# Batch 0 of a fused two-layer kernel, planned anew: order of loads, two transpose banks, slabs turned one step ahead

## The chip, the cores and the metric

One core of one Trainium2 chip. The time is the device time of one launch in microseconds, as the median of several runs. Beside it stands a profile: one execution recorded by the hardware, whose times count from the start of its span. The engines are PE (TensorE: matmuls and transposes), DVE (VectorE), ACT (ScalarE), POOL (GpSimd) and SP (SyncE, which issues DMAs here). Each runs its own list of instructions in order and waits on semaphores. PEld is TensorE's load of weights, which runs beside its matmuls.

## The reference

```python
def _L0_cond_ref(hidden_states, W, b, coeff, mask):
    output = jnp.einsum('bsi,oi->bso', hidden_states, W) + b
    sign = (2 * mask - 1).astype(hidden_states.dtype)
    diff = jnp.einsum('bsi,bio->bso', hidden_states, sign)
    return output + diff * coeff[:, None, None]

def _L1_cond_ref(x, adapter_ids, base_weight, base_bias, lora_A_w, lora_B_w):
    result = jnp.einsum('bsd,od->bso', x, base_weight) + base_bias
    A = lora_A_w[adapter_ids]
    Bw = lora_B_w[adapter_ids]
    h = jnp.einsum('bsd,brd->bsr', x, A)
    return result + jnp.einsum('bsr,bor->bso', h, Bw)

x = x + _L0_cond_ref(x, L0_cond_W, L0_cond_b, condB_coeff, mask)
x = x + _L1_cond_ref(x, itok, L1_cond_base_weight, L1_cond_base_bias, lora_A_w, lora_B_w)
```

x is 8 batches of 256 x 1024 in float32, the mask is 8 x 1024 x 1024 int32, both weights are 1024 x 1024, and the adapters have rank 16.

## The kernel before

The work is 64 steps, 8 for each batch b; step n makes chunk c = n mod 8, which is 128 of the 1024 columns of the first layer. For one step ACT turns the mask chunk into signs (`sign`), DVE makes the weight W0 + coeff * sign + identity (`make_w`), and the two split it into a high and a low part (`chunk_hi` on ACT, `chunk_lo` on DVE), so that two fast matmuls replace a full-precision one. PE multiplies them with the split x (`layer1`, k = 0 to 7). ACT and DVE read the sum from PSUM, add the bias (`half_y`, `make_y`) and split it (`y_parts_hi`, `y_parts_lo`). One step later PE multiplies it with the adapters (`adapter_h`) and with chunk n of the second weight (`layer2`, four groups of three matmuls). After 8 steps ACT and DVE split the adapter's result h (`h_parts_hi`, `h_parts_lo`), PE adds its product (`finish`), and the output leaves (`move_z`, `store_z`).

Weights arrive in rows and are needed in columns. So PE transposes them in batch 0, in units of four 128 x 128 transposes into one PSUM bank (`turn_unit`): 16 units of W0, 16 of W1, 4 of the first x, 2 each of adapters A and B. The list `units` gives kind, chunk, half and bank. POOL adds the identity to a slab before it is turned (`eye_w0`, `eye_w1`); ACT copies a turned W0 unit out (`copy_w0`), and ACT and DVE split the turned W1, A and B (`split_hi`, `split_lo`). From step 1 on all units share bank 7 (`TB`). The split x of the next batch is made by DVE transposes of 32 x 32 blocks (`turn_rows`, into the single buffer xt), `rows_hi` on ACT and `rows_lo` on DVE, two halves g = 0 and 1; the layer1 of the next batch needs them.

The order on each engine is the order in which the code is written. SP issues loads in order on one queue and waits before each for the buffer's last reader; POOL issues the later W0 slabs and the gathered adapters. From batch 1 on only masks and x are loaded, and no unit is turned.

```python
    for n in range(1, KT):
        if n + 2 < KT:
            units += [("w0", n + 2, h, TB) for h in range(2)]
        if n == 6:
            units += [("b", 0, h, TB) for h in range(2)]
        units += [("w1", n, h, TB) for h in range(2)]
```

## Time and profile before

| | us |
|---|---|
| median of 3 runs | 437.23 (435.9 to 437.77) |
| the profiled execution, its time | 436.89 |
| its span | 435.2 |
| PE busy | 407.3 (94%) |
| DVE busy | 283.1 (65%) |
| ACT busy | 237.4 (55%) |
| POOL busy | 25.2 (6%) |

The span is what the recorded instructions cover; 1.69 us of the execution's time lie around it. Busy shares are means over stages that differ: batch 0, with the loads and transposes, and the seven others. A row of the trace gives a start, a duration, engine, line, operation, what it writes and reads, how many in a row, and in brackets the idle time before it with what ended it.

### The profile page before, as it was taken

The page shows a single profiled execution, that of the slowest core. Times are in us where ns is not written, and L with a number is a line of the kernel's source. Part 1 is how long each engine was busy: PE and PEld are TensorE (multiplying, and loading weights), DVE is VectorE, ACT ScalarE, POOL GpSimd, SP SyncE. Part 2 cuts the span into 40 slices and gives each one's busy share as a digit, 9 for nine tenths or more (in the row PEclk, how much of TensorE's full clock was granted, in tenths as well). Part 3 has the DMA queues.
Part 4 walks back from the last instruction along what each step waited for, and adds up shares of the span by engine and source line. Part 5 has one row for each costly group of instructions (what it writes and reads, how often), then busy time and mean ns, then how long its engine had stood idle before and what let it go on. Part 6 is the DMA issues. An engine that isn't in the chain of part 4 may idle for free.

```text
span 435.2 us, 5517 instructions
## 1 busy us (share of the span) xinstructions
PE 407.3 (94%) x2049; PEld 341.0 (78%) x2049; DVE 283.1 (65%) x334; ACT 237.4 (55%) x352; POOL 25.2 (6%) x47
## 2 busy tenths in 40 slices
PE   3649999788999999999999999999999999999996
PEld 3538878566888888888888888888888888888885
DVE  0455757786578756886578657876588658865512
ACT  3366666636555645665455754565565555665412
POOL 4334410000000000000000000000000000000000
PEclk9997999999999999999999999999999999999999
DMA  7995694615973299218942496319911793246002
GB/s 232 244 331 157 211 229 134 146 48 128 217 175 98 76 201 234 69 39 203 228 125 62 122 234 165 98 48 224 243 52 50 185 251 104 77 116 163 2 0 97
DMA packets 90846, 63.29 MB, mean 145 GB/s; under 512 B 3515, under 2 KB 84419, under 8 KB 90820
## 3 DMA queue, kind: packets, MB, share of 16 engines
q1 hardware_dynamic: 89588, 59.28, 55.5%
q0 software_dynamic: 1232, 3.67, 2.5%
q8 instruction: 16, 0.26, 0.2%
q14 instruction: 10, 0.08, 0.1%
HBM read 51.39 MB, written 8.39 MB: 137 GB/s over the span
## 4 chain that ended last, share of the span: by engine, by line
PE 82%; DMA 5%; DVE 5%; SPq 4%; ACT 2%; issue 1%; ACTq 0%; DVEq 0%
PE ps L631 25%; PE ps L633 13%; PE ps L658 13%; PE ps L657 12%; PE ps L659 12%; DMA wm<-in_mask_Bx4096x_ik_dram 5%; PE ps L641 3%; PE ps L617 2%; PE ps L669 2%; SPq L183 1%; DVE wm L499 1%; DVE w1lo L471 1%; SPq L190 1%; DVE wlo L505 1%; SPq L226 1%
## 5 line engine op out<-in xcount | busy, mean ns | idle before, releaser
L631 PE MATMUL ps<-xhl,whi 128*128 128x512 f32 x512 | 187.6, 405 | 1.9 <-DVE wlo L505 1.1
L633 PE MATMUL ps<-xhl,wlo 128*128 128x256 f32 x512 | 144.9, 283 | 0.0
L631 PEld LDWEIGHTS ps<-xhl,whi 128*128 128x128 f32 x512 | 97.8, 191 | 24.9 <-DVE wlo L505 1.3
L505 DVE TENSOR_TENSOR wlo<-wm,whi 128x1024 fp32r<-128x1024 f32 x64 | 79.2, 1238 | 48.6 <-ACT whi L351 48.6
L351 ACT ACTIVATE whi<-wm 128x1024 fp32r<-128x1024 f32 x64 | 67.8, 1059 | 75.0 <-DVE wm L499 73.7
L657 PE MATMUL ps<-w1hi,yhl 128*128 128x512 f32 x256 | 101.5, 396 | 0.0
L658 PE MATMUL ps<-w1lo,yhl 128*128 128x512 f32 x256 | 100.6, 393 | 0.0
L659 PE MATMUL ps<-w1hi,yhl 128*128 128x512 f32 x256 | 100.4, 392 | 0.0
L633 PEld LDWEIGHTS ps<-xhl,wlo 128*128 128x128 f32 x512 | 98.1, 192 | 2.4
L499 DVE SCALAR_TENSOR_TENSOR wm<-wm,cs,w0t 128x1024 f32<-128x1024 f32 x64 | 81.6, 1275 | 23.4 <-ACT w0t L329 12.4
L344 ACT ACTIVATE wm<-wm 128x1024 f32<-128x1024 int32 x64 | 67.4, 1054 | 9.6 <-DMA wm<-in_mask_Bx4096x_ik_dram 9.5
L659 PEld LDWEIGHTS ps<-w1hi,yhl 128*128 128x128 f32 x256 | 48.1, 188 | 10.6
L658 PEld LDWEIGHTS ps<-w1lo,yhl 128*128 128x128 f32 x256 | 48.1, 188 | 10.5
L657 PEld LDWEIGHTS ps<-w1hi,yhl 128*128 128x128 f32 x256 | 48.2, 188 | 7.8
L515 DVE TENSOR_TENSOR yhl<-ysum,yhl 128x256 fp32r<-128x256 f32 x64 | 27.3, 427 | 36.6 <-ACT yhl L384 36.5
L377 ACT ACTIVATE ysum<-ps,b0col 128x256 f32<-128x256 f32 x64 | 30.0, 468 | 33.6 <-PE ps L633 33.2
L511 DVE TENSOR_TENSOR ysum<-ps,ysum 128x256 f32<-128x256 f32 x64 | 26.9, 420 | 13.8 <-ACT ysum L377 13.7
L362 ACT ACTIVATE xhl<-xt 128x1024 fp32r<-128x1024 f32 x14 | 14.9, 1061 | 31.1 <-DVE xt L476 31.1
L384 ACT ACTIVATE yhl<-ysum 128x256 fp32r<-128x256 f32 x64 | 26.4, 413 | 8.4 <-DVE ysum L511 8.2
L476 DVE STREAM_TRANSPOSE xt<-xraw 128x1024 f32<-128x1024 f32 x14 | 30.6, 2183 | 0.0
L641 PE MATMUL ps<-yhl,at 128*128 128x512 f32 x64 | 25.4, 397 | 0.0
L617 PE MATMUL ps<-ident,w0raw 128*128 128x128 f32 x64 | 11.6, 320 | 10.8 <-POOL w0raw L262 5.4
(49 smaller groups left out, 186.9 us busy)
## 6 DMA issues: line engine op xcount, KB each, us to landing
wm<-in_mask_Bx4096x_ik_dram SPq DMA_DIRECT2D x64, 512.0 KB, 5.7
out_dram<-zst SPq DMA_DIRECT2D x32, 256.0 KB, 2.5
xraw<-in_x_dram SPq DMA_DIRECT2D x28, 256.0 KB, 7.3
w1raw<-_L_cond_base_weight_dram SPq DMA_DIRECT2D x8, 512.0 KB, 6.2
bt<-bhl SPq DMA_DIRECT2D x48, 64.0 KB, 2.9
w0raw<-in_L_cond_W_dram POOLq DMA_DIRECT2D x5, 512.0 KB, 6.9
w0raw<-in_L_cond_W_dram SPq DMA_DIRECT2D x3, 512.0 KB, 8.6
xrows<-in_x_dram SPq DMA_DIRECT2D x2, 512.0 KB, 6.6
```

The lines of the kernel that those rows point to most:

```text
L344: nc.scalar.activation(wm[:, s, :], wm[:, s, :].bitcast(I32), ACT.Copy, bias=-1.0, scale=2.0).then_inc(sign_made, 1)
L351: nc.scalar.activation(whi[:, n % WS, :, :], wm[:, n % MS, :].rearrange("p (k o) -> p k o", k=KT), ACT.Copy).then_inc(w_hi, 1)
L377: nc.scalar.activation(ysum[:, n % 2, :], ps[:, L1B + n % 2, S:2 * S], ACT.Identity, bias=b0col[:, n % KT:n % KT + 1]).then_inc(y_half, 1)
L476: nc.vector.transpose(xt[:, :, :].rearrange("p t (n q) -> p n t q", q=Q), xraw[:, :, :].rearrange("p n (i k) -> p n k i", k=KT)[:, :, g * ...
L499: nc.vector.scalar_tensor_tensor(chunk, chunk, cs[:, b:b + 1], w0t[:, c, :, :].rearrange("p k o -> p (k o)"), ALU.mult, ALU.add).then_inc( ...
L505: nc.vector.tensor_tensor(wlo[:, s, :, :], wm[:, n % MS, :].rearrange("p (k o) -> p k o", k=KT), whi[:, s, :, :].bitcast(F32), ALU.subtrac ...
L631: nc.tensor.matmul(ps[:, bank, :], whi[:, s, k, :], xhl[:, b % 2, k, :], start=(k == 0), stop=False, skip_group_check=True)
L633: op = nc.tensor.matmul(ps[:, bank, 0:S], wlo[:, s, k, :], xhl[:, b % 2, k, 0:S], start=False, stop=(k == KT - 1), skip_group_check=True)
L641: op = nc.tensor.matmul(ps[:, HB, :], at[:, c, b * 2 * R:b * 2 * R + P], yhl[:, n % 2, :], start=(c == 0), stop=(c == KT - 1))
L657: nc.tensor.matmul(ps[:, Z0 + j, :], hi, w1hi[:, c, cols], start=(c == 0), stop=False)
L658: nc.tensor.matmul(ps[:, Z0 + j, :], hi, w1lo[:, c, cols], start=False, stop=False)
L659: op = nc.tensor.matmul(ps[:, Z0 + j, :], lo, w1hi[:, c, cols], start=False, stop=False)
```

## The change

1. **Loads.** The small loads (coefficients, first bias, adapter ids, second bias) leave SP's queue for ACT's, ahead of ACT's first work. All W0 slabs go on SP's queue, each just ahead of its mask; POOL keeps the gathered adapters, A in two parts (5 and 3 of 8) with a slab's identity between.
2. **Banks.** Units from step 1 on alternate over banks 5 and 7 by half, and the two W1 units 0 use banks 2 and 3. In return layer1 has one bank (4) in batch 0 and waits for the `make_y` of the step before (`l1_bank`).
3. **Order in batch 0.** In step n PE turns W0 slab n + 1 (before: n + 2), the first half after two k and the second after four. After step 0 it turns W1 before A. B is turned in step 4, not 6. The bias transpose comes first of all on PE. The order on ACT and DVE follows: chunk n + 1 is made in step n.
4. **x.** The first x is turned g by g, and layer1 of step 0 starts at the first g. Second batch: the DVE transposes come at the end of steps 5 and 6 (before 4 and 6), half 1 first, `rows_hi` in steps 6 and 7, and the low part is made by POOL (`second_rows_lo`), the first of them ahead of `eye_w1(7)`. Layer1 of a later batch waits for both halves at its start; `load_x` comes at c == 3 rather than 2.
5. **Bias.** The two parts of the second bias are made by POOL, not by ACT and DVE.

```diff
@@ units and banks
-    Z0, L1B, HB, TB = 0, 4, 6, 7
+    Z0, L1B, HB, TB = 0, 4, 6, (5, 7)
...
-        if n + 2 < KT:
-            units += [("w0", n + 2, h, TB) for h in range(2)]
-        if n == 6:
-            units += [("b", 0, h, TB) for h in range(2)]
-        units += [("w1", n, h, TB) for h in range(2)]
+        if n + 1 < KT:
+            units += [("w0", n + 1, h, TB[h]) for h in range(2)]
+        if n == 4:
+            units += [("b", 0, h, TB[h]) for h in range(2)]
+        units += [("w1", n, h, TB[h]) for h in range(2)]
...
-        return 4 + 2 * (b - 1) + g + 1
+        return 4 + 2 * (b - 1) + 2 - g
+
+    def first_split(st, g):
+
+        return 2 * g + st + 1
+
+    def l1_bank(n):
+        return L1B if n < KT else L1B + (n + 1) % 2
@@ SP
             for n in range(NS):
                 b, c = divmod(n, KT)
+                if n + 4 < KT:
+                    load_w0(n + 4)
                 if n + 4 < NS:
                     load_mask(n + 4)
...
-                if n == 7:
+                if n == 5:
                     load_bt(0)
...
-                if c == 2 and b + 1 < NB:
+                if c == 3 and b + 1 < NB:
                     load_x(b + 1)
@@ POOL
+            def second_rows_lo(g):
+                pool.wait_ge(x_hi, x_split(1, g))
+                k = slice(g * TG, (g + 1) * TG)
+                nc.gpsimd.tensor_tensor(xhl[:, 1, k, S:2 * S], xt[:, :, :], xhl[:, 1, k, 0:S].bitcast(F32),
+                                        ALU.subtract).then_inc(x_lo, 1)
...
             eye_w0(4)
             eye_w1(2)
+            pool.wait_ge(b1_in, 16)
+            nc.gpsimd.tensor_copy(b1hi[:, :], b1raw[:, :]).then_inc(bias_hi, 1)
+            pool.wait_ge(bias_hi, 1)
+            nc.gpsimd.tensor_tensor(b1lo[:, :], b1raw[:, :], b1hi[:, :].bitcast(F32), ALU.subtract).then_inc(bias_lo, 1)
             eye_w0(5)
+            eye_w1(3)
             load_b()
-            load_w0(7)
-            eye_w1(3)
             eye_w0(6)
+            eye_w1(4)
...
-            eye_w1(4)
             eye_w0(7)
             eye_w1(5)
             eye_w1(6)
+            second_rows_lo(1)
             eye_w1(7)
+            second_rows_lo(0)
@@ ACT
+            act.dma_start(cs[:, :], coeff.rearrange("(e b) -> e b", e=1).to_broadcast([P, NB])).then_inc(coeff_in, 16)
+            act.dma_start(b0row[:, :], b0.rearrange("(c p) -> c p", p=P)).then_inc(b0_in, 16)
+            act.dma_start(id_row[:, :], ids.rearrange("(e b) -> e b", e=1)).then_inc(ids_in, 16)
+            act.dma_start(b1raw[:, :], b1.rearrange("(e o) -> e o", e=1)).then_inc(b1_in, 16)
...
+            for n in range(1, KT):
+                if n + 1 < KT:
+                    copy_w0(n + 1, 0)
+                    copy_w0(n + 1, 1)
+                if n == 4:
                     split_hi("b", 0, 0)
...
+                half_y(n)
+                chunk_hi(n + 1)
+                y_parts_hi(n)
                 split_hi("w1", n, 0)
...
+                if n >= 6:
+                    rows_hi(1, 7 - n)
+                sign(n + 2)
+                if n == 7:
+                    chunk_hi(9)
+                    sign(10)
@@ DVE
+            for n in range(1, KT):
+                make_w(n + 1)
+                if n == 4:
                     split_lo("b", 0, 0)
...
+                make_y(n)
+                chunk_lo(n + 1)
+                y_parts_lo(n)
                 split_lo("w1", n, 0)
                 split_lo("w1", n, 1)
...
+                if n in (5, 6):
+                    turn_rows(1, 6 - n)
+                if n == 7:
+                    make_w(9)
+                    chunk_lo(9)
@@ PE
+                if n + 1 < KT:
+                    layer1(n, range(0, 2))
+                    turn_unit("w0", n + 1, 0)
+                    layer1(n, range(2, 4))
+                    turn_unit("w0", n + 1, 1)
+                    if n == 4:
+                        layer1(n, range(4, 6))
                         turn_unit("b", 0, 0)
-                    layer1(n, range(3, 6))
...
+                        layer1(n, range(6, 8))
                         turn_unit("b", 0, 1)
...
```

The order of the instructions at three places. First SP's queue at its start, before (in_L_cond_W is W0, in_mask the mask, base_weight W1, in_x the first x; the small ones are ids, coefficients and biases):

```order
1 L218 DMA id_row<-in_itok_B_15_dram 1x8
2 L183 DMA w0raw<-in_L_cond_W_dram 128x1024
3 L171 DMA wm<-in_mask_Bx4096x_ik_dram 128x8x128
4 L222 DMA xrows<-in_x_dram 128x1024 x2
5 L223 DMA cs<-in_condB_coeff_dram 128x8
6 L183 DMA w0raw<-in_L_cond_W_dram 128x1024
7 L171 DMA wm<-in_mask_Bx4096x_ik_dram 128x8x128
8 L226 DMA b0row<-in_L_cond_b_dram 8x128
9 L190 DMA w1raw<-in_L_cond_base_weight_dram 128x8x128
10 L183 DMA w0raw<-in_L_cond_W_dram 128x1024
```

and the same place of the changed kernel:

```order
1 L194 DMA w0raw<-in_L_cond_W_dram 128x1024
2 L179 DMA wm<-in_mask_Bx4096x_ik_dram 128x8x128
3 L232 DMA xrows<-in_x_dram 128x1024 x2
4 L194 DMA w0raw<-in_L_cond_W_dram 128x1024
5 L179 DMA wm<-in_mask_Bx4096x_ik_dram 128x8x128
6 L201 DMA w1raw<-in_L_cond_base_weight_dram 128x8x128
7 L194 DMA w0raw<-in_L_cond_W_dram 128x1024
8 L179 DMA wm<-in_mask_Bx4096x_ik_dram 128x8x128
9 L201 DMA w1raw<-in_L_cond_base_weight_dram 128x8x128
10 L194 DMA w0raw<-in_L_cond_W_dram 128x1024
```

Three small loads are gone from between the large ones, and the large ones keep their order up to the third mask.

Second, ACT from the end of step 6 to the start of the adapter's result h, changed kernel (L375 is rows_hi of the second batch's x, L357 sign, L390 half_y, L364 chunk_hi, L397 y_parts_hi, L352 split_hi, L405 h_parts_hi):

```order
55 L375 ACTIVATE xhl<-xt 128x4x256
56 L357 ACTIVATE wm<-wm 128x1024
57 L390 ACTIVATE ysum<-ps,b0col 128x256
58 L364 ACTIVATE whi<-wm 128x1024
59 L397 ACTIVATE yhl<-ysum 128x256
60 L352 ACTIVATE w1hi<-ps 128x512 x2
61 L375 ACTIVATE xhl<-xt 128x4x256
62 L357 ACTIVATE wm<-wm 128x1024
63 L364 ACTIVATE whi<-wm 128x1024
64 L357 ACTIVATE wm<-wm 128x1024
65 L364 ACTIVATE whi<-wm 128x1024
66 L390 ACTIVATE ysum<-ps,b0col 128x256
```

In the kernel before, the first of the two rows_hi stood in step 5, and the second in step 7 (row 72 here) between the two W1 halves:

```order
68 L384 ACTIVATE yhl<-ysum 128x256
69 L344 ACTIVATE wm<-wm 128x1024
70 L377 ACTIVATE ysum<-ps,b0col 128x256
71 L339 ACTIVATE w1hi<-ps 128x512
72 L362 ACTIVATE xhl<-xt 128x4x256
73 L351 ACTIVATE whi<-wm 128x1024
74 L339 ACTIVATE w1hi<-ps 128x512
```

So the second half of x moves from ahead of step 7's last weight chunk to behind all of step 7's splits, and the first half a step later.

Third, the end of POOL's list, changed kernel (L272 and L278 add the identity to a W0 and a W1 slab, L296 is second_rows_lo):

```order
88 L278 TENSOR_TENSOR w1raw<-w1raw,ident 128x128
89 L328 COPY bsort<-abraw 128x1024
90 L272 TENSOR_TENSOR w0raw<-w0raw,ident 128x128
91 L278 TENSOR_TENSOR w1raw<-w1raw,ident 128x128 x2
92 L296 TENSOR_TENSOR xhl<-xt,xhl 128x4x256
93 L278 TENSOR_TENSOR w1raw<-w1raw,ident 128x128
94 L296 TENSOR_TENSOR xhl<-xt,xhl 128x4x256
```

In the kernel before no such row is on POOL; the two subtractions are DVE's L482.

## Rows read from the trace of the kernel before

**Rows 1.** Windows: us, busy of PE, PEld, DVE, ACT, POOL, clock, DMA share, GB/s.

```profile
0.00:35.00 35.00, 17.65 (x87) 15.43 (x88) 12.72 (x17) 17.42 (x26) 12.31 (x26) 0.94 1.01 270
...
102.50:431.40 328.90, 328.82 (x1637) 276.52 (x1635) 223.47 (x262) 179.22 (x263) 0.00 (x0) 1.00 0.55 132
```

**Rows 2.** One of PE's waits in the first 104 us: total, times, longest.

```profile
PE ps L617 <- DVE bhl L471: 2.7, 2, 1.9
```

**Rows 3.** Timeline of the start: start, us, engine, line, operation.

```profile
4.82 0.45 POOL L262 TENSOR_TENSOR w0raw<-w0raw,ident 128x128 f32<-128x128 f32 x1 [1.41 <-DMA w0raw<-in_L_cond_W_dram]
...
8.72 3.67 PE L617 MATMUL ps<-ident,xrows 128*128 128x128 f32 x16 [1.36 <-DMA xrows<-in_x_dram]
...
10.94 1.28 DVE L499 SCALAR_TENSOR_TENSOR wm<-wm,cs,w0t 128x1024 f32<-128x1024 f32 x1 [10.94 <-DMA cs<-in_condB_coeff_dram]
...
14.34 0.48 POOL L280 DMA_DIRECT2D abraw<-in_L_cond_lora_A_w_dram  x1 [0.65 <-issue]
...
16.52 0.24 PE L680 MATMUL ps<-ident,b0row 8*128 8x8 f32 x1 [4.12 <-DVE xhl L489]
...
18.62 0.46 POOL L268 TENSOR_TENSOR w1raw<-w1raw,ident 128x128 f32<-128x128 f32 x1 [3.32 <-DMA w1raw<-_L_cond_base_weight_dram]
```

**Rows 4.** PE's timeline in steps 1 to 8, and ACT's last weight split before the adapter.

```profile
32.91 1.12 PE L617 MATMUL ps<-ident,w0raw 128*128 128x128 f32 x4 [5.34 <-DVE w1lo L471]
...
34.46 0.63 PE L631 MATMUL ps<-xhl,whi 128*128 128x512 f32 x1
...
35.10 0.63 PE L631 MATMUL ps<-xhl,whi 128*128 128x512 f32 x1
...
41.99 0.40 PE L631 MATMUL ps<-xhl,whi 128*128 128x512 f32 x1
...
42.34 0.40 PE L631 MATMUL ps<-xhl,whi 128*128 128x512 f32 x1
...
45.68 0.39 PE L641 MATMUL ps<-yhl,at 128*128 128x512 f32 x1
...
49.80 0.40 PE L631 MATMUL ps<-xhl,whi 128*128 128x512 f32 x1
...
97.64 1.06 ACT L351 ACTIVATE whi<-wm 128x1024 fp32r<-128x1024 f32 x1 [4.25 <-DVE wm L499]
...
100.84 0.94 PE L669 MATMUL ps<-bt,ht 128*128 128x512 f32 x3 [1.57 <-ACT ht L395]
...
102.54 0.40 PE L631 MATMUL ps<-xhl,whi 128*128 128x512 f32 x1
```

**Rows 5.** Costliest groups of the page: times, busy us, mean ns.

```profile
L505 DVE TENSOR_TENSOR wlo<-wm,whi 128x1024 fp32r<-128x1024 f32 x64 | 79.2, 1238 | 48.6 <-ACT whi L351 48.6
L351 ACT ACTIVATE whi<-wm 128x1024 fp32r<-128x1024 f32 x64 | 67.8, 1059 | 75.0 <-DVE wm L499 73.7
...
L499 DVE SCALAR_TENSOR_TENSOR wm<-wm,cs,w0t 128x1024 f32<-128x1024 f32 x64 | 81.6, 1275 | 23.4 <-ACT w0t L329 12.4
...
L476 DVE STREAM_TRANSPOSE xt<-xraw 128x1024 f32<-128x1024 f32 x14 | 30.6, 2183 | 0.0
```

**Rows 6.** DMA issues: KB each, median us to landing.

```profile
abraw<-in_L_cond_lora_A_w_dram POOLq DMA_DIRECT2D x8, 64.0 KB, 7.3
abraw<-in_L_cond_lora_B_w_dram POOLq DMA_DIRECT2D x8, 64.0 KB, 2.3
...
bt<-b1lo SPq DMA_DIRECT2D x1, 4.0 KB, 5.7
```

**Rows 7.** Two operations of POOL's timeline, B's loads and B's splits as groups.

```profile
27.04 1.50 POOL L262 TENSOR_TENSOR w0raw<-w0raw,ident 128x128 f32<-128x128 f32 x1
...
50.92 1.11 POOL L316 COPY bsort<-abraw 128x1024 f32<-128x1024 f32 x1
...
L287 POOL DMA_DIRECT2D abraw<-in_L_cond_lora_B_w_dram x8 | 4.3, 542 | 5.2 <-issue 5.2
...
L339 ACT ACTIVATE bhl<-ps 128x512 fp32r<-128x512 f32 x2 | 2.4, 1198 | 2.7 <-PE ps L617 2.7
```

More of the change, by code:

```diff
@@ L268, in eye_w1, with load_a @@
                 nc.gpsimd.tensor_tensor(diag, diag, ident[:, :], ALU.add).then_inc(w1_eyed, 1)
-            def load_w0(c):
-                s = c % W0S
-                pool.wait_ge(unit_turned, number["w0", c - W0S, 1] + 1)
-                pool.dma_start(w0raw[:, s, :], W0[c * P:(c + 1) * P, :]).then_inc(w0_in[c], 16)
-            def load_a():
-                pool.wait_ge(ids_in, 16)
-                for e in range(NB):
+            def load_a(adapters):
+                for e in adapters:
                     name = pool.value_load(id_row[0:1, e:e + 1], min_val=0, max_val=NL - 1)
@@ L405, in _ @@
             sign(0)
-            first_rows_hi(0, 0)
             chunk_hi(0)
-            first_rows_hi(0, 1)
-            first_rows_hi(1, 0)
-            first_rows_hi(1, 1)
+            for g in range(2):
+                for st in range(ST):
+                    first_rows_hi(st, g)
+            copy_w0(1, 0)
             sign(1)
-            copy_w0(1, 0)
             copy_w0(1, 1)
@@ L415, in _ @@
             chunk_hi(1)
-            for n in range(KT):
-                if n == 0:
-                    sign(2)
-                if n + 2 < KT:
-                    copy_w0(n + 2, 0)
-                if n == 6:
-                    split_hi("b", 0, 0)
-                if n > 0:
-                    sign(n + 3)
-                if n + 2 < KT:
-                    copy_w0(n + 2, 1)
-                if n == 6:
-                    split_hi("b", 0, 1)
-                if n > 0:
-                    half_y(n)
-                if n == 0:
-                    sign(3)
-                    split_hi("a", 0, 0)
-                    split_hi("a", 0, 1)
+            y_parts_hi(0)
+            split_hi("w1", 0, 0)
+            split_hi("w1", 0, 1)
+            split_hi("a", 0, 0)
+            split_hi("a", 0, 1)
+            sign(2)
+            for n in range(1, KT):
[3 more added lines that the diff above has]
+                if n == 4:
+                    split_hi("b", 0, 0)
+                    split_hi("b", 0, 1)
+                half_y(n)
+                chunk_hi(n + 1)
+                y_parts_hi(n)
                 split_hi("w1", n, 0)
-                if n in (5, 7):
-                    rows_hi(1, (n - 5) // 2)
-                chunk_hi(n + 2)
                 split_hi("w1", n, 1)
-                y_parts_hi(n)
-                if n == 1:
-                    act.wait_ge(b1_in, 16)
-                    nc.scalar.activation(b1hi[:, :], b1raw[:, :], ACT.Copy).then_inc(bias_hi, 1)
+                if n >= 6:
[4 more added lines that the diff above has]
+                    sign(10)
             for n in range(KT, NS):
@@ L446, in _ @@
                 if c in (5, 7) and b + 1 < NB:
[L447 removed]
+                    rows_hi(b + 1, 1 - (c - 5) // 2)
                 if n + 2 < NS:
@@ L590, in turn_unit @@
                 before = [v for v in range(u) if units[v][3] == bank]
-                if u == number["w1", 0, 0]:
-                    pe.wait_ge(b0_moved, 1)
                 if before and units[before[-1]][0] == "x":
-                    pe.wait_ge(x_lo, 4)
+                    pe.wait_ge(x_lo, first_split(*units[before[-1]][1:3]))
                 elif before and units[before[-1]][0] == "w0":
@@ L621, in layer1 @@
                 b, c = divmod(n, KT)
-                bank = L1B + n % 2
+                bank = l1_bank(n)
                 s = n % WS
@@ L625, in layer1 @@
                     pe.wait_ge(w_lo, n + 1)
-                    if n >= 2:
+                    if n == 0:
+                        pe.wait_ge(b0_moved, 1)
+                    elif n < KT:
+                        pe.wait_ge(y_made, n)
+                    else:
                         pe.wait_ge(y_made, n - 1)
+                    if n == KT:
+                        pe.wait_ge(parts_lo, parted(number["w1", KT - 1, 0]))
+                    if c == 0 and b > 0:
+                        pe.wait_ge(x_lo, x_split(b, 0))
                 for k in ks:
-                    if c == 0 and k % TG == 0:
-                        pe.wait_ge(x_lo, x_split(b, k // TG) if b else 4)
+                    if n == 0 and k % TG == 0:
+                        pe.wait_ge(x_lo, first_split(ST - 1, k // TG))
                     nc.tensor.matmul(ps[:, bank, :], whi[:, s, k, :], xhl[:, b % 2, k, :],
```

117 lines of the change are left out of this document (44 added, 73 removed).

## The prediction

> **What bounds the kernel now.** I read the windows first. From 102.5 us to 431.4 us PE is busy 328.82 of 328.90 us at full granted clock [rows 1]: seven batches in which PE is the bound and no load or split is waited for. The change moves almost nothing there, so whatever it is worth shows in one number, the start of layer1 of step 9, 102.54 us now [rows 4]. PE's total of 407.3 us less those 328.8 leaves 78.5 us of work before it, so some 24 us there are waits. The list of waits and the timeline name the largest: 5.34 us for the low part of a W1 unit in step 1 [rows 4], 2.7 us for that of B [rows 2], at the start some 5 us until the first slab is ready at 4.82, and 4.12 us in which PE has turned x and waits for its last low part [rows 3].
>
> Second, the clock. After the 5.34 us wait that ends at 32.91, a pair of layer1 matmuls starts every 0.64 us, later every 0.35 us [rows 4]: the lower and the upper of the two levels (1.2 and 2.4 GHz). PE reaches its first matmul of step 2 only at 41.99. From there a step with two W0 and two W1 units takes 7.81 us, 3.69 of it layer1 with its units, 4.12 layer2 with its own [rows 4].
>
> Third, the loads. In the first 35 us the DMA engines are busy throughout and move 270 GB/s [rows 1], which is 9.45 MB, 18 slabs of 0.52 MB at 1.9 us each. So in that stretch order counts, not the queue: the slab that is used first should be ahead.
>
> **The start, part by part.** All times from here are of the changed kernel, placed one after another by the durations above.
>
> Without the ids ahead, W0 slab 0 lands 0.4 us earlier, so PE turns it from about 5.0 (now its identity is added at 4.82 [rows 3]). The bias row now stands first on PE; its load is issued on a queue of its own at about 2 us, and I cost it at nothing, covered by the slab; if it lands later than 5, each us late is a us. Chunk 0's weight waited until 10.94 for the coefficients, which lay behind 2 MB on SP's queue [rows 3]. On ACT's queue they are early, and it starts behind the sign at about 8.65. With 1.28, 1.06 and 1.24 us for make, high and low [rows 5] the low part is there at 12.2. The first g of x (16 transposes from 8.72 take 3.67 us now [rows 3]) is split behind it: 13.5. So layer1 of step 0 starts at about 13.5, against 16.7 behind the bias transpose at 16.52 [rows 3]. If its first 4 us run at the lower level, like the stretch that follows 32.91 [rows 4], it ends near 19.
>
> W1 slab 0 is ready near 18.3 (18.62 now [rows 3]), its units are turned at 20. Then comes A. Its last load is issued at 14.34 now; a slab's identity stands between the parts now and waits for W0 slab 1 (about 12), so I place it at 15.4, and with 7.3 us to landing [rows 6] A is there at 22.7. Layer1 of step 1 starts at 23.6, not delayed by the weight (its low part is there at 22.2). Two k, a unit that waits until 24.45 for A's low part, and the rest: layer1 ends at 27.45, layer2 at 31.4. That is step 2's start, against 41.99 [rows 4]. The slabs it needs are the tenth to thirteenth of the 18, in order of use, so at 1.9 us each they land by 27. The 5.34 us wait goes, since W0 slab 2's units no longer stand behind W1's in one bank.
>
> **Steps 2 to 7.** With two banks a W1 unit no longer waits for the split of the other half. Now that costs 0.2 us a step: eight pairs of 0.35 us leave 0.89 of layer1's 3.69 for two units; a pair is 768 columns, so the 13 matmuls of 512 in layer2 take 3.03, and with 0.89 that is 3.92 of 4.12. Without it a step is 7.62. The single layer1 bank costs nothing: its last reader `make_y` is one of two short operations behind layer1, an estimated 1 us, and layer2 covers it for 3.9. Chunk n + 1 is made in step n: the unit is turned at +2.3, the copy and `make_w` end at +4.2, but `chunk_hi` stands behind `half_y` on ACT and ends at +5.25, the low part at +6.45. That is 1.1 us before it is needed. So step 3 starts at 39.0, step 4 at 46.6.
>
> In step 4 B is turned. POOL reaches its loads when W1 slab 3 has landed (about 37.5), and they take 4.3 + 5.2 us of issue [rows 7], 2.3 to land [rows 6], and 1.1 us for the sorting copy [rows 7]: 50.7. PE wants B at 49.6, so 1.1 us late. Its high part also waits for the bias rows, which SP issues behind W1 slab 5, from 46.4; at 3 to 5.7 us to landing [rows 6] they are there at 51 to 53.6, I take 51.5. Behind it stand two splits of 1.2 us each on ACT [rows 7], and behind them `half_y` and chunk 5. So step 5 starts at 56.8 (an undisturbed one: 46.6 + 7.62 + 0.87 for B's two units = 55.1). Step 6: 64.4, step 7: 72.0. The x transposes on DVE fit into gaps of 2.2 us at the ends of steps.
>
> **The x of batch 1.** Here a wait is added. Both halves pass one buffer in series, and the chain now runs over POOL. `rows_hi` of half 1 stands behind the last W1 split of step 6 and ends at 73.0. POOL's subtraction takes D. Then DVE's transpose of half 0, 2.18 us, then `make_w` of chunk 8, 1.28, behind it on DVE, then `chunk_hi`, 1.06 [rows 5], `y_parts_hi` and two W1 splits on ACT, short ones that I estimate at 1.4 together, then `rows_hi`, 1.06, and D once more. Layer1 of step 8 waits for both halves: 73.0 + 2.2 + 1.3 + 1.1 + 1.4 + 1.1 + 2D = 80.1 + 2D. PE itself would be there at 72.0 + 6.7 = 78.7.
>
> D has no row. Bounds: 1.11 us, POOL's copy of as many elements with one input [rows 7], and 3.6 us, eight times the 0.45 us of an addition with an eighth of the elements [rows 3]. I take 2.2, twice the copy, as there are two inputs. That gives 84.5 and a wait of 5.8 us. The Trainium skill speaks against this move: its page GPSIMD Engine Reference, section Elementwise, side-by-side cycle accounting, gives a two-input float32 operation 1.96 times VectorE's time and keeps VectorE as the rule for such work. By it D would be 1.96 x 1.24 = 2.4 us, an estimate, and the sum 0.4 us more. No row here has the operation on POOL.
>
> After a wait like that I expect the lower clock again, as after 5.34 us [rows 4]: layer1 takes 4.8 instead of 2.8 us. It hides behind the next chain. `sign(9)` and chunks 9 and 10 stand behind the second `rows_hi`; DVE makes chunk 9 once POOL is through (84.4), and 1.28 + 1.06 + 1.24 + 1.28 later chunk 10 is made: its `chunk_hi` starts at 89.3. From that operation to `finish` it is 3.2 us now (97.64 to 100.84 [rows 4]): 92.5. Then 1.7 us, as now, to layer1 of step 9: about 94.0.
>
> **Sum.** 102.54 - 94.0 = 8.5 us off the profiled execution's 436.89: 428.4. The median of the runs is 0.3 us above that one, so 428.7. Behind step 9 I expect no change: PE waits for nothing there [rows 1], the halves of x only change places, and that layer1 now wants both at its start moves the need of the second forward by four pairs, 1.4 us; the cover is the step between the split and that start, and if it is gone it costs up to 1.4 us in each of seven batches.
>
> **Rivals.** (1) *Nothing waits as I count it.* D near 1.11, bias rows and A early. The chain then ends at 82.3, A gives 1.5 us, B 1.2: about 13 us, 424. For it: the measured copy [rows 7]. Against: two inputs. (2) *The start gives less.* In the wait for A (20.0 to 22.7) the clock may fall, 2 us; a slab order in which each load is 1 us later than counted delays step 2 by as much; ACT's four issues may hold its first copy by 1 us. Gain 4 to 5 us: 433. For it: the clock did fall over the 5.34 us wait [rows 4]. Against: this wait is half as long, nearer to that of 1.9 us for B [rows 2]. (3) *Slower, by POOL's subtraction.* The end of the chain moves by 2D. The gain is gone at D = 2.2 + 8.5/2 = 6.4 us, and it is slower by over 0.5% from about 7.5. One row shows how: an addition that takes 0.45 us alone took 1.50 us beside a DVE operation [rows 7], 3.3 times as long. If POOL's pass stretched by that, D = 7.3 and the time 439. Against: DVE waits for the first pass itself, and the stretch in the row is about the length of one DVE operation, not a factor. (4) *The change does nothing that counts*: step 8 is reached earlier, but x's chain and the adapter's hold step 9 where it was, within 2 us of now. It needs 6 us lost in steps 4 to 8 beyond the above.
>
> **Chances.** Forecast (426 to 431) 0.50; rival 1 0.16; rival 2 0.21; rival 4 0.07; rival 3 0.06. Half a per cent of this kernel's time, 2.2 us, is about what a measurement can tell from no change. Faster 0.87, same 0.07, slower 0.06. The range takes in rivals 1 and 2: 423 to 434.5.
>
> **What would show it.** In the changed profile: the first `make_w` at 8.7 rather than 10.94; layer1 of step 0 near 13.5; step 2 near 31.4 with no wait over 3 us ahead of it; steps of 7.6 us; a wait of about 1 us for B in step 4; POOL's two long subtractions of about 2.2 us; a wait of PE of about 6 us before layer1 of step 8, ended by POOL's second; step 9 at 94. The prediction is wrong if A or the loads hold PE beyond 24 us at step 1, if POOL's work delays DVE in steps 2 and 3, where the slack is only 1.1 us, or if a stretch behind step 9 is not as it was.

## The result

The changed kernel takes 435.1 us (median of 20 runs, 432.85 to 437.67) against 437.42 us before (20 runs beside it): a ratio of 0.995, 95% interval 0.9934 to 0.9966. That is 2.3 us, half a per cent, where 8.5 were forecast. The profiled execution took 432.9 us, the second fastest of these 20, so the 4.0 us between its span of 431.2 us and the 435.2 of before is more than the typical gain.

The list of PE's waits in the first 104 us of the changed kernel (total, times, longest) answers to [rows 2]:

```profile
PE ps L688 <- DMA b0row<-in_L_cond_b_dram: 6.0, 1, 6.0
PE ps L645 <- POOL xhl L296: 5.6, 1, 5.6
PE ps L623 <- POOL bsort L328: 2.7, 1, 2.7
PE ps L623 <- DMA abraw<-in_L_cond_lora_A_w_dram: 2.6, 1, 2.6
PE ps L623 <- DMA xrows<-in_x_dram: 2.2, 2, 2.1
```

The wait of 5.34 us of [rows 4] is gone. PE now waits 5.6 us for x of batch 1, 2.7 for B's sorting copy and 2.6 for A. Before, it waited 0.8 us for x, 2.7 in all for B's low parts, and not for A. The timeline (start, us, engine, line, operation, wait before it) places them; it answers to [rows 3] and [rows 4], and L645 is `layer1`:

```profile
6.28 0.45 POOL L272 TENSOR_TENSOR w0raw<-w0raw,ident 128x128 f32<-128x128 f32 x1 [2.87 <-DMA w0raw<-in_L_cond_W_dram]
...
15.66 0.76 PE L645 MATMUL ps<-xhl,whi 128*128 128x512 f32 x1 [0.72 <-DVE xhl L501]
...
25.13 1.09 PE L623 MATMUL ps<-ident,abraw 128*128 128x128 f32 x8 [2.65 <-DMA abraw<-in_L_cond_lora_A_w_dram]
25.98 0.48 PE L645 MATMUL ps<-xhl,whi 128*128 128x512 f32 x1
...
34.18 0.40 PE L645 MATMUL ps<-xhl,whi 128*128 128x512 f32 x1
...
49.37 0.39 PE L645 MATMUL ps<-xhl,whi 128*128 128x512 f32 x1
...
55.20 0.63 PE L623 MATMUL ps<-ident,bsort 128*128 128x128 f32 x4 [2.67 <-POOL bsort L328]
...
61.26 0.40 PE L645 MATMUL ps<-xhl,whi 128*128 128x512 f32 x1
...
89.26 0.76 PE L645 MATMUL ps<-xhl,whi 128*128 128x512 f32 x1 [5.59 <-POOL xhl L296]
...
98.70 0.39 PE L645 MATMUL ps<-xhl,whi 128*128 128x512 f32 x1
```

The rows of L645 that carry a step's start, set against the forecast:

| start of layer1 of step | forecast | profiled | late | a second execution (r1_same) |
|---|---|---|---|---|
| 0 | 13.5 | 15.66 | 2.2 | 15.59 |
| 1 | 23.6 | 25.98 | 2.4 | 26.03 |
| 2 | 31.4 | 34.18 | 2.8 | 34.68 |
| 4 | 46.6 | 49.37 | 2.8 | 49.84 |
| 5 | 56.8 | 61.26 | 4.5 | 64.67 |
| 7 | 72.0 | 76.43 | 4.4 | 79.85 |
| 8 | 84.5 | 89.26 | 4.8 | 92.65 |
| 9 | 94.0 | 98.70 | 4.7 | 102.06 |

Behind step 9 nothing moved: 431.2 - 98.70 = 332.5 us, against 435.2 - 102.54 = 332.7 before. The difference sits in two rows of this table, steps 0 and 5; between them the steps run at nearly the forecast pace. Of the other times that the forecast named, the first `make_w` came at 10.69 us, not at 8.7, since the sign and the slab ahead of it were late; PE waited for A until 25.13, beyond the 24 that the forecast had set as a sign of being wrong. The last column is the same kernel again, with 3.4 us more, of which 2.9 arise between steps 4 and 5.

### The profile page after: what moved, and what is told of

It is laid out like the page before. It is cut to its first block, busy times and chain, and to the rows that moved or that the text cites. A ratio compares the mean times of both kernels' runs of the same rounds, so it can differ in the third digit from the quotient of the medians.

```text
span 431.2 us, 5519 instructions
## 1 busy us (share of the span) xinstructions
PE 406.1 (94%) x2049; PEld 342.0 (79%) x2049; DVE 280.4 (65%) x331; ACT 237.1 (55%) x351; POOL 29.6 (7%) x46
## 4 chain that ended last, share of the span: by engine, by line
PE 82%; DMA 6%; issue 5%; POOL 3%; POOLq 2%; DVE 1%; ACT 1%; DVEq 0%; ACTq 0%
PE ps L645 25%; PE ps L647 13%; PE ps L672 13%; PE ps L671 13%; PE ps L673 12%; PE ps L655 3%; DMA w1raw<-_L_cond_base_weight_dram 2%; PE ps L683 2%; DMA abraw<-in_L_cond_lora_A_w_dram 2%; DMA w0raw<-in_L_cond_W_dram 1%; PE ps L623 1%; DMA abraw<-in_L_cond_lora_B_w_dram 1%; POOLq L282 1%; POOL xhl L296 1%; POOLq L65 1%
## 5 line engine op out<-in xcount | busy, mean ns | idle before, releaser
L645 PE MATMUL ps<-xhl,whi 128*128 128x512 f32 x512 | 188.2, 406 | 6.3 <-POOL xhl L296 5.6
L645 PEld LDWEIGHTS ps<-xhl,whi 128*128 128x128 f32 x512 | 98.1, 192 | 29.6 <-issue 7.1
L364 ACT ACTIVATE whi<-wm 128x1024 fp32r<-128x1024 f32 x64 | 67.8, 1060 | 78.4 <-DVE wm L511 76.7
L511 DVE SCALAR_TENSOR_TENSOR wm<-wm,cs,w0t 128x1024 f32<-128x1024 f32 x64 | 83.1, 1298 | 20.3 <-ACT w0t L342 15.5
L357 ACT ACTIVATE wm<-wm 128x1024 f32<-128x1024 int32 x64 | 67.4, 1053 | 4.9 <-DMA wm<-in_mask_Bx4096x_ik_dram 4.7
L672 PEld LDWEIGHTS ps<-w1lo,yhl 128*128 128x128 f32 x256 | 48.2, 188 | 10.6
L390 ACT ACTIVATE ysum<-ps,b0col 128x256 f32<-128x256 f32 x64 | 29.9, 468 | 36.8 <-PE ps L647 36.7
L375 ACT ACTIVATE xhl<-xt 128x1024 fp32r<-128x1024 f32 x14 | 14.8, 1061 | 31.0 <-DVE xt L488 31.0
L397 ACT ACTIVATE yhl<-ysum 128x256 fp32r<-128x256 f32 x64 | 26.3, 412 | 8.5 <-DVE ysum L523 8.2
L342 ACT ACTIVATE w0t<-ps 128x512 f32<-128x512 f32 x16 | 9.6, 598 | 12.4 <-PE ps L623 12.3
```

The lines of the kernel that those rows point to most:

```text
L357: nc.scalar.activation(wm[:, s, :], wm[:, s, :].bitcast(I32), ACT.Copy, bias=-1.0, scale=2.0).then_inc(sign_made, 1)
L364: nc.scalar.activation(whi[:, n % WS, :, :], wm[:, n % MS, :].rearrange("p (k o) -> p k o", k=KT), ACT.Copy).then_inc(w_hi, 1)
L390: nc.scalar.activation(ysum[:, n % 2, :], ps[:, l1_bank(n), S:2 * S], ACT.Identity, bias=b0col[:, n % KT:n % KT + 1]).then_inc(y_half, 1)
L511: nc.vector.scalar_tensor_tensor(chunk, chunk, cs[:, b:b + 1], w0t[:, c, :, :].rearrange("p k o -> p (k o)"), ALU.mult, ALU.add).then_inc( ...
L645: nc.tensor.matmul(ps[:, bank, :], whi[:, s, k, :], xhl[:, b % 2, k, :], start=(k == 0), stop=False, skip_group_check=True)
L672: nc.tensor.matmul(ps[:, Z0 + j, :], hi, w1lo[:, c, cols], start=False, stop=False)
```

## The experiments

All are edits of the changed kernel. The first eight ran in two sets (before: 437.22 and 437.19 us), the last four in one (before: 437.33 us).

| run | edit | median us | ratio to before, 95% | step 9 at |
|---|---|---|---|---|
| r1_same | none | 435.21 | 0.9939 (0.9913 to 0.9966) | 102.06 |
| r2_small_late | small loads behind slab 0 | 436.05 | 0.9985 (0.9962 to 1.0008) | 101.26 |
| r3_b_step5 | B turned in step 5 | 430.42 | 0.9838 (0.9798 to 0.9877) | 97.12 |
| r4_x_low_dve | x's low part back on DVE | 433.63 | 0.9899 (0.9865 to 0.9933) | 100.06 |
| r5_x_early | x chain earlier | 432.72 | 0.9886 (0.9834 to 0.9939) | 98.55 |
| r6_a_first | all of A first | 434.81 | 0.9939 (0.9909 to 0.9969) | 100.18 |
| r7_start_between | small loads on SP's queue behind slab 0 | 435.37 | 0.9951 (0.9921 to 0.998) | 99.59 |
| r8_b5_x_early | r3 and r5 | 429.84 | 0.9819 (0.9756 to 0.9881) | 94.93 |
| r9_h_first | r8, h's parts ahead of chunk 10 | 426.69 | 0.976 (0.9719 to 0.98) | 90.28 |
| r10_h_first_a | r9 and r6 | 427.38 | 0.9765 (0.9723 to 0.9807) | 90.26 |
| r11_h_alone | h's parts ahead of chunk 10 | 437.35 | 0.9995 (0.9968 to 1.0023) | 100.66 |
| r12_cs_one_row | coefficients to one row | 434.51 | 0.993 (0.9903 to 0.9957) | 100.11 |

### The same kernel again

> The changed kernel once more, unaltered, as the yardstick of this call and a second profile of it. The median of its 20 runs, 435.1 us, is 2.2 us above its profiled execution (432.9). Theory S (the start varies from run to run, by when the first slabs land): this profile shows step 2 and step 9 at another time than 33.9 and 98.7 us, by 1 to 3 us, and the difference arises before step 2. Rival T (the other runs lose time behind step 9): step 9 stands at 98.7 within 0.5 us, whatever the time. Time expected 435.1, ratio to before 0.995.

No edit. The median of 435.21 us repeats the first one. In this execution, at 436.29 us, PE waited as long for A as in the other (2.63 against 2.65 us), and afterwards the clock was at its lower level. Two rows of its timeline, and its windows (busy of PE, PEld, DVE, ACT, POOL, clock, DMA share, GB/s):

```profile
24.57 1.81 PE L623 MATMUL ps<-ident,abraw 128*128 128x128 f32 x8 [2.63 <-DMA abraw<-in_L_cond_lora_A_w_dram]
...
56.45 1.08 PE L623 MATMUL ps<-ident,bsort 128*128 128x128 f32 x4 [3.45 <-POOL bsort L328]
```

```profile
24.00:30.00 6.00, 5.43 (x28) 5.06 (x29) 1.69 (x3) 3.12 (x5) 0.91 (x2) 0.72 1.11 327
...
52.00:62.00 10.00, 6.55 (x28) 5.52 (x26) 3.54 (x4) 4.01 (x5) 2.76 (x6) 0.68 0.79 173
```

The eight transposes of A take 1.81 us instead of 1.09. In the other execution the clock stood at 1.00 in both windows. So about the same wait for A was followed by the upper level (2.4 GHz) once and by the lower (1.2 GHz) once. The two are not alike ahead of it, though: this one had also waited 1.37 us for W1 slab 0 at 20.88, and the first had not. What the waits cost is more than their length: here the B wait is 0.8 us longer, and with what follows it step 5 starts 3.4 us later.

Neither theory of the expectation came true: the difference does not arise before step 2, nor behind step 9, but at B. Of the 32 executions of this kernel the slower ones mostly have the lower mean granted clock (0.990 in those at 432.57 and 432.9 us, 0.978 at 437.67). That fits a fall of the clock as the reason why the median lies 2.2 us above the first profiled time, but only two of them have a trace.

### The small loads at the start

> Only the adapter ids are issued at once on ACT's queue; coefficients and both biases are issued there after W0 slab 0 has landed, and the bias transpose goes back behind the units of x on PE. Theory L (the four small loads beside slab 0 are what makes it land at 6.28 instead of 4.4): POOL's first addition comes at 4.4 to 4.9 us, PE's first transposes at 5.0 to 5.4, step 2 about 1.5 us earlier than in the unaltered kernel of the same call, and the time 1 to 2 us less. Rival (chance, or mask and x on SP's own queue are what slows slab 0): the first addition stays between 5.5 and 6.5, and the time is the same within 0.5 us. A third way: the slab is early but A's adapters still arrive at 25, as DMA is full until then, and the time stays.

```diff
             act.dma_start(id_row[:, :], ...)
+            act.wait_ge(w0_in[0], 16)
             act.dma_start(cs[:, :], ...)
             act.dma_start(b0row[:, :], ...)
             act.dma_start(b1raw[:, :], ...)
```

The bias transpose goes behind x on PE, and `b0col` behind `make_w(0)` on DVE. Slab 0's identity starts at 4.43 us instead of 6.28. But the coefficients are then late, layer1 of step 0 starts at 18.60 after 4.56 us of waiting for x's low part, and the time is 436.05 us, where 1 to 2 us less than the changed kernel were expected. The window of 2 to 4 us shows what the small loads had done, first of the changed kernel, then of this one:

```profile
2.00:4.00 2.00, 0.00 (x0) 0.00 (x0) 0.00 (x0) 1.28 (x1) 1.41 (x3) 1.00 0.55 167
```

```profile
2.00:4.00 2.00, 0.00 (x0) 0.00 (x0) 0.00 (x0) 0.00 (x0) 1.42 (x3) 1.00 0.81 281
```

> The changed kernel with coefficients and first bias issued on SP's queue straight behind mask 0, ahead of x, the second bias behind mask 3, and only the ids on ACT's queue; the bias transpose stands behind x's units on PE, as in the kernel before. Against the version in which they waited for slab 0 (slab at 4.43, but coefficients late, layer1 of step 0 at 18.6) theory L says that both can be had: first identity at 4.4, first make_w below 9.5 us, layer1 of step 0 at 13.5 to 14, step 2 about 1.8 us earlier than in the changed kernel, time 1.5 to 2.5 us less. Rival H (the small loads cost as much wherever they stand, now x or mask 0 lands later): layer1 of step 0 stays at 15 or later and the time within 0.7 us.

```diff
+            sp.dma_start(cs[:, :], ...)      # behind load_w0(0), load_mask(0)
+            sp.dma_start(b0row[:, :], ...)
             for st in range(ST):
                 sp.dma_start(xrows[:, st, :], ...)
```

The second bias goes on SP's queue behind mask 3; PE and DVE are ordered as in the run before. Slab 0's identity is at 4.44 and the first `make_w` at 8.67 us, both as in the forecast. Now the first x pays: its units start at 10.84 after 3.85 us of waiting, the window of 6 to 8 us moves 127 GB/s, and layer1 of step 0 starts at 17.37. The time is 435.37 us, that of the changed kernel, as the rival in the expectation had it.

> The changed kernel with the coefficients loaded into one row of 32 bytes instead of 128 rows of 32 bytes, and ones set in their place (each batch's coefficient is 1, so the values differ). It asks what of the small loads delays slab 0. Theory P (their 128 small packets of the coefficients do, of 164 on that queue): the first identity starts at 4.4 to 4.8 us instead of 6.28, and layer 1's first product at about 13.8 to 14.5 instead of 15.66; the time is 433.5 to 434.8. Rival T (the queue is what costs, the set-up of four transfers beside slab 0, not the packets): identity at 6.0 to 6.4, no change of time.

```diff
-            act.dma_start(cs[:, :], coeff.rearrange("(e b) -> e b", e=1).to_broadcast([P, NB]))
+            act.dma_start(cs_row[:, :], coeff.rearrange("(e b) -> e b", e=1))
...
+            nc.vector.memset(cs[:, :], 1.0)
```

This settles which of the small loads costs. The run leaves out the spread of the coefficients over 128 rows: ones are set in their place, so its values differ, and its other work is the same. ACT's queue now carries 22 packets instead of 164, the other three loads unchanged, and slab 0 is not delayed. Its timeline:

```profile
4.83 1.97 PE L625 MATMUL ps<-ident,w0raw 128*128 128x128 f32 x8 [0.15 <-POOL w0raw L273]
...
13.46 0.47 PE L647 MATMUL ps<-xhl,whi 128*128 128x512 f32 x1 [0.74 <-DVE xhl L502]
...
22.78 1.97 PE L625 MATMUL ps<-ident,abraw 128*128 128x128 f32 x8 [2.96 <-DMA abraw<-in_L_cond_lora_A_w_dram]
...
54.59 1.09 PE L625 MATMUL ps<-ident,bsort 128*128 128x128 f32 x4 [3.44 <-POOL bsort L329]
```

Three times of the forecast come out to 0.2 us: slab 0's units (forecast 5.0), layer1 of step 0 (13.5), A (22.7). So the load of the coefficients, one row of 32 bytes for each of 128 partitions and 142 of that queue's 164 packets, is the cause of the 2.2 us. And yet the time is only 434.51 us, an interval that overlaps that of the unaltered kernel: what PE gained, it waits at B, 3.44 us, with the lower clock behind it (0.66 in the window of 52 to 62 us).

### A

> The changed kernel with all eight loads of A ahead of W0 slab 1's identity on GpSimd, instead of five ahead and three behind. Theory E (A's last load waits behind that slab, and PE's 2.6 to 3.1 us wait for A follows it): the last load is issued 1.4 us earlier, the wait shrinks by as much, step 2 comes 1.4 us earlier, or 3 us where the clock then stays up; time 1 to 3 us less. Rival F (the identity of slab 1 is now late for PE, at about 17 against 16.4, and chunk 1 behind it): the wait only moves to W0 slab 1 or to chunk 1, and the time is the same within 0.7 us. Rival G (A's arrival is set by the load on the DMA engines, not by its issue): the last load is earlier and PE's wait for A ends at 24.5 to 25 as before.

```diff
-            load_a(range(0, 5))
+            load_a(range(0, NB))
             eye_w0(1)
-            load_a(range(5, NB))
```

The wait for A falls from 2.65 to 0.41 us and the clock stays up in the window of 24 to 30 us. In its place PE waits 0.29 us for slab 1, 0.64 for chunk 1 and 1.17 for A's low part, and then 3.70 for B. 434.81 us: no gain.

### B

> B's two units, their splits and the row loads that use them come one step later (step 5 instead of 4). Theory W (the 2.67 us wait for B's sorting copy and what stands behind it are real time on the path): no wait for the sorting copy, step 6 and step 9 about 3 us earlier, time 2.5 to 3 us less than the unaltered kernel. Rival X (what step 4 loses is covered later, since the x chain holds layer1 of step 8): the chain moves with step 6, whose W1 split stands ahead of it, so the rival needs x to be held by its load, issued behind W1 slab 5; then the time falls by under 1 us.

```diff
-        if n == 4:
+        if n == 5:
             units += [("b", 0, h, TB[h]) for h in range(2)]
```

The same step in the orders of ACT, DVE and PE; `load_bt(0)` in n == 6. No wait for B is left, only 0.2 us for a low part and 0.4 for B's own. 430.42 us, 4.8 less than r1_same, the largest effect of one edit and more than the 2.5 to 3 us expected. It did not need the start to be better: PE still waits 3.07 us for A there. POOL's timeline of the changed kernel shows why B is late in step 4:

```profile
35.53 2.38 POOL L321 TENSOR_TENSOR b1lo<-b1raw,b1hi 1x1024 fp32r<-1x1024 f32 x1
37.87 1.43 POOL L272 TENSOR_TENSOR w0raw<-w0raw,ident 128x128 f32<-128x128 f32 x1
39.27 0.45 POOL L278 TENSOR_TENSOR w1raw<-w1raw,ident 128x128 f32<-128x128 f32 x1
39.68 0.58 POOL L291 DMA_DIRECT2D abraw<-in_L_cond_lora_B_w_dram  x1
...
46.82 0.53 POOL L291 DMA_DIRECT2D abraw<-in_L_cond_lora_B_w_dram  x1 [0.61 <-issue]
50.53 0.53 POOL L291 DMA_DIRECT2D abraw<-in_L_cond_lora_B_w_dram  x1 [3.18 <-issue]
...
54.02 1.04 POOL L328 COPY bsort<-abraw 128x1024 f32<-128x1024 f32 x1 [2.06 <-DMA abraw<-in_L_cond_lora_B_w_dram]
```

### The x of batch 1

> The two low parts of the second batch's x are made by VectorE again, at the same places (ends of steps 6 and 7), not by GpSimd; nothing else moves. GpSimd's two passes took 2.41 and 2.35 us. Theory P (the passes are in series in front of layer1 of step 8, so each counts fully): 1.2 us saved on each, the wait before layer1 of step 8 falls from 5.6 to 3.2 us, step 9 2.4 us or more earlier (one weight chunk on VectorE took 2.53 instead of 1.28 us beside the second pass, 1.2 us more), time 2.4 to 3.6 us less. Rival Q (VectorE becomes the bound there, its other work waits instead): under 1 us less, or more time.

```diff
-            second_rows_lo(1)
             eye_w1(7)
-            second_rows_lo(0)
...
+                if n >= 6:
+                    rows_lo(1, 7 - n)      # DVE
```

The wait before layer1 of step 8 falls from 5.6 to 4.13 us, and the time to 433.63, 1.6 us less than r1_same where 2.4 to 3.6 were expected. Two passes of 2.4 us on POOL became two of 1.23 and 1.22 on DVE, so of 2.3 us saved 1.5 reach the wait; there they queue behind DVE's other work. POOL's passes in the changed kernel, and the `make_w` that DVE ran beside the second:

```profile
77.56 2.41 POOL L296 TENSOR_TENSOR xhl<-xt,xhl 128x1024 fp32r<-128x1024 f32 x1 [11.51 <-ACT xhl L375]
...
86.76 2.35 POOL L296 TENSOR_TENSOR xhl<-xt,xhl 128x1024 fp32r<-128x1024 f32 x1 [6.38 <-ACT xhl L375]
```

```profile
80.07 2.14 DVE L488 STREAM_TRANSPOSE xt<-xraw 128x1024 f32<-128x1024 f32 x1 [2.81 <-POOL xhl L296]
...
87.66 2.53 DVE L511 SCALAR_TENSOR_TENSOR wm<-wm,cs,w0t 128x1024 f32<-128x1024 f32 x1 [0.41 <-ACT wm L357]
```

> The changed kernel with only the x of batch 1 reordered: DVE's transposes at the ends of steps 4 and 6, half 1's high part at the end of step 5 and its low part on GpSimd behind the last W1 identity, half 0's high part on ACT straight behind half_y of step 7 and its low part on DVE straight behind make_y, both ahead of chunk 8. Theory P (the series transpose, high, low twice, with chunk 8 and the W1 splits between, is all that holds layer1 of step 8): the wait of 5.6 us before layer1 of step 8 falls below 1 us, and with it the stretch at the lower clock behind it; step 9 comes 5.5 to 7.5 us earlier, time 428 to 430. Rival Q (chunk 8 and the adapter's chain only wait in its place, as finish stands behind chunk 10): a wait of 2 to 4 us appears before step 8 or finish and the time falls by 2 to 3.5 us only.

```diff
                 half_y(n)
+                if n == 7:
+                    rows_hi(1, 0)          # ACT, ahead of chunk_hi(8)
                 chunk_hi(n + 1)
...
+                if n == 5:
+                    rows_hi(1, 1)
```

DVE turns half 1 in step 4 and makes the low part of half 0 ahead of `chunk_lo(8)`; POOL keeps the low part of half 1, behind its last identity. Layer1 of step 8 now waits only 1.61 us, for a W1 unit, and runs at the upper clock. But the first `finish` waits 2.95 us for `ht`, and 432.72 us is 2.5 less than r1_same, not the 5 to 7 expected: the wait moved on to `ht`, as rival Q had it. B's wait (3.83) and A's (3.40) came with low clocks in this one (0.66 and 0.72 in the two windows).

> B one step later and the x of batch 1 reordered, together. Theory: B's wait and x's wait are in series on PE, so what the two gave alone adds up (4.8 us, and what the x order gives alone, expected 5.5 to 7.5): 424 to 426. Rival: step 5 now holds B's splits and x's high part together on ACT and a transpose of x on DVE just before, and the sum falls short by 1 to 3 us with a wait in step 5 or 6.

Both edits, nothing else: 429.84 us, only 0.6 less than B's alone and above the 424 to 426 expected. Its timeline shows the wait that took the place of the one for x, and the 0.62 us matmuls at the lower clock behind it:

```profile
84.34 0.47 PE L648 MATMUL ps<-xhl,whi 128*128 128x512 f32 x1 [1.60 <-DVE w1lo L484]
...
92.65 0.94 PE L686 MATMUL ps<-bt,ht 128*128 128x512 f32 x3 [3.01 <-ACT ht L407]
93.42 0.43 PE L674 MATMUL ps<-w1hi,yhl 128*128 128x512 f32 x1
93.66 0.62 PE L675 MATMUL ps<-w1lo,yhl 128*128 128x512 f32 x1
```

ACT's timeline names what it stood behind: chunk 10's `chunk_hi` at 89.45, which had itself waited for DVE, then `half_y`, then `ht`:

```profile
89.45 1.06 ACT L363 ACTIVATE whi<-wm 128x1024 fp32r<-128x1024 f32 x1 [1.54 <-DVE wm L512]
90.42 0.46 ACT L389 ACTIVATE ysum<-ps,b0col 128x256 f32<-128x256 f32 x1
90.77 0.36 ACT L404 ACTIVATE ht<-ps 32x256 fp32r<-32x256 f32 x1
```

### The adapter's h

> B's units in step 5 and the x chain early, as in the run that joined those two (429.84, with a wait of 3.01 us of the first finish for ht, and low-clock pairs of 0.63 behind it), and now the parts of batch 0's h ahead of chunk 10 on ACT and on VectorE. Theory (Q: the wait that was taken from the x chain stood again at ht, because ht's copies stood behind make_w(10), chunk_hi(10) and half_y(8)): the adapter's product ends near 87.6 us, ht follows within 2 us, finish waits under 0.7 us and the clock stays at 1.00 behind it; 3.0 less 0.5 of wait and about 1.0 of low clock go: 426 to 427 us. Rival R: the next thing behind is chunk 10 or y of chunk 8, now late, and step 9 or 10 waits for them as long: 429 to 430.

```diff
             for n in range(KT, NS):
...
+                if n == KT:
+                    h_parts_hi(0)          # ACT, ahead of chunk_hi(10)
                 if n + 2 < NS:
                     chunk_hi(n + 2)
...
+                if n == KT:
+                    h_parts_lo(0)          # DVE, ahead of make_w(10)
```

`ht` is copied from 86.98 on, `finish` starts without a wait at 88.70, and step 9 at 90.28, 12.3 us earlier than before. 426.69 us, within the 426 to 427 expected, 10.6 us less than before, 8.5 less than the changed kernel (r1_same) and the best of all here. Not all 12.3 arrive, since 424.8 - 90.28 = 334.5 us lie behind step 9 instead of 332.5. Its timeline has waits there that the changed kernel's does not have:

```profile
99.53 0.50 PE L663 MATMUL ps<-yhl,at 128*128 128x512 f32 x1 [0.31 <-DVE yhl L531]
138.02 0.93 PE L691 MATMUL ps<-bt,ht 128*128 128x512 f32 x3 [0.95 <-ACT ht L407]
```

> As the run before it, and also all eight loads of A ahead of slab 1's identity. Theory: the wait for A of some 2.6 us becomes under 0.6 us, but chunk 1 and slab 1 of W0 wait about that much, as when this was done alone, and B's wait stays gone; the time is within 0.7 us of the run before it. Rival: with B's wait gone the start is what is left, and a step 1 without a low clock brings 1 to 2 us: 425.

All of A first again on top: PE's wait for A is 1.54 us instead of 2.50 with the clock up, but it waits 0.95 for A's low part and 1.66 instead of 0.40 us for B's. 427.38 us, not to be told from the run before it.

> The changed kernel with nothing but the parts of batch 0's h ahead of chunk 10 on both engines. Theory Q again: there chunk 10 is made while TensorE waits 5.6 us for the x chain, so nothing stands ahead of ht when it is wanted, and finish waits under 0.7 us with or without this edit: 435.2, within 0.5 us. Rival: the copies of h are late by themselves at the end of batch 0, and the edit brings 1 us or more.

The expectation of no change missed: 437.35 us. `finish` has no wait, as the theory said, but the edit has a price of its own: 435.5 - 100.66 = 334.8 us behind step 9, 2.3 more than the 332.5 of the changed kernel, and 2.3 is about what the median lies above it. Chunk 10 is made later: its high part starts 7.6 us behind layer1 of step 8 (99.79 - 92.21), in the changed kernel 4.5 (93.77 - 89.26). PE then waits for ACT and DVE at three places, 1.5 us together, the last at the end of the next batch. That the delayed chunk is what they are behind with is argued from these rows. The waits:

```profile
109.78 0.50 PE L660 MATMUL ps<-yhl,at 128*128 128x512 f32 x1 [0.33 <-DVE yhl L530]
116.03 0.50 PE L660 MATMUL ps<-yhl,at 128*128 128x512 f32 x1 [0.22 <-DVE yhl L530]
...
148.60 0.92 PE L688 MATMUL ps<-bt,ht 128*128 128x512 f32 x3 [0.97 <-ACT ht L408]
```

The same execution has a wait of PE that the others do not have. In steps 2 and 3 POOL's `b1lo` and a subtraction of DVE stretched beside each other (rows at the end), a W1 low part came late, and PE waited for it:

```profile
39.27 0.71 PE L628 MATMUL ps<-ident,w0raw 128*128 128x128 f32 x4 [2.01 <-DVE w1lo L486]
```

Step 4 then starts at 53.87 instead of 49.37, so B's sorting copy, at 54.52, is there when PE wants it. The forecast had named this delay, POOL's work holding DVE in steps 2 and 3, as a sign of being wrong.

## Why the prediction was wrong

- **Start.** Wrong in the term "I cost it at nothing, covered by the slab". The term was said of the bias row, and the coefficients beside it got no term at all; their load costs slab 0 1.9 us (4.32 against 6.28 for its identity). Layer1 of step 0 came at 15.66, not 13.5, and A at 25.1, not 22.7. With the coefficients in one row the trace gives the forecast times. I had looked at when the small loads land, not at what they do to the large one beside them. By itself this term is worth little: r12 won the 2.2 us back at the start and 0.6 in the time.
- **B.** The step that failed most is "50.7. PE wants B at 49.6, so 1.1 us late". Its own terms add up to 50.4, so 0.8 us late; B was sorted at 55.06. POOL reached its loads at 39.68 instead of 37.5, because the bias's `b1lo`, 2.38 us, stood ahead of them with an identity that took 1.43 us, which I had not counted; issuing took 11.4 us instead of 9.5 (a pause of 3.18 us before the last load); landing took 0.7 us more. The bias rows, which the forecast put last at 51.5, held nothing here: ACT's split of B waited for PE. Moving B by a step brought 4.8 us.
- **The clock behind A's and B's waits.** I had it as part of a rival, for A only. Behind waits of 2.4 to 3.8 us it fell in some executions and stayed up in others. The mean clock is lower in most of the slower executions over the spread from 432.6 to 437.7 us, so it is the likely reason for most of the distance from the profiled time to the median; that is not shown, and the kernel before spreads as widely (435.82 to 439.56) without these two waits.
- **Pace.** Right: steps of 7.6 us, and no wait of 5.34 us.
- **x of batch 1.** Right to 0.3 us in its length: from the end of the first `rows_hi` to layer1 of step 8 it took 89.26 - 77.48 = 11.8 us against 11.5, with D = 2.41 and 2.35 for the assumed 2.2, and PE waited 5.59 for 5.8. The 2.2 was a guess between two bounds, and that it came out so near was luck. The two-input factor named from the Trainium skill, GPSIMD Engine Reference, section Elementwise, side-by-side cycle accounting, gave an estimate of 2.4 us, and the trace agrees with it. The lower clock came, and `finish` 7.8 us behind layer1 of step 8, against 8.0.
- **Rivals.** The result lies between rival 2, 433, and no change. Its mechanism came in both parts, though not always together: the start was later than counted, and the clock fell in A's wait in the second profile, not in the first. It left out B. Rival 3's stretched pass did not come: D was 2.41 with DVE idle and 2.35 with DVE busy, and it was DVE's `make_w` that stretched, from 1.28 to 2.53 us.
- **Behind step 9.** Right, 332.5 against 332.7 us.

Together: 2.4 us at the start, 0.4 to step 2, 1.7 at B and 0.2 at x make the 4.7 us by which step 9 was late, and 0.2 us fewer lie behind it, so 432.9 instead of 428.4. The other 2.2 us lie between this execution and the median, and the clock is their likely reason.

Where the gain went: PE reached A and B earlier, and neither came earlier for it. They stand behind loads and behind POOL's list: B's sorting copy started between 53.4 and 56.6 us in all the changed kernels, whether layer1 of step 0 had started at 13.5 or at 18.6. The chain of x is another kind of bound. It hangs on PE's own pace, through the W1 splits of steps 6 and 7: from layer1 of step 7 to that of step 8 it took 12.8 us in all eight profiles that leave x alone (after, r1, r2, r3, r6, r7, r11, r12), wherever step 7 started between 74.81 and 79.85. So it costs a fixed wait of 5.6 us and passes on what is gained ahead of it. The six of them with B in step 4 and h untouched (after, r1, r2, r6, r7, r12) all take 369.9 to 370.0 us from layer1 of step 5 to the end of the span. Their spans differ only by when step 5 starts, and in all but r2 PE waits for B just ahead of it.

With B and x moved, the next wait was the one for `ht`. Against r1_same B alone brought 4.8 us, x alone 2.5, h alone cost 2.1, and the three together brought 8.5 (10.6 against the kernel before). What stays open: why POOL pauses 2.5 to 4.8 us before B's eighth load (3.2 in the changed kernel's profile), and whether a spread of the coefficients that needs no 128 packets would bring more once B no longer holds PE; neither was tried.

## What to carry to other kernels

When a prologue is re-planned, list for every item the time at which it can be there at the earliest, with all that its queue issues and computes before it, and compare that with the new time of need: the gain ends at the first item that is not earlier. Ask of each such wait whether it has a time of its own or a fixed distance behind the waiting engine, as x has here: the first swallows what is gained ahead of it, the second passes it on. Such waits can stand in series, so removing one alone can show little or nothing: one alone brought 4.8 us, 2.5 or a loss of 2.1 here, the three together 8.5. A small load is not small by its bytes; count its rows, and see what large load runs beside them.
